# Edge counts of a graph layer in three narrow groups of tiles per window in place of one wide group

## The reference, cut to what matters

```python
xr = jnp.einsum('nd,rdf->rnf', x, W)
oi = xr[etype, dst]
oj = xr[etype, src]
qi = oi @ q
kj = oj @ k
alpha = jax.nn.leaky_relu(qi + kj, NEG_SLOPE)
m = jax.ops.segment_max(alpha, dst, num_segments=n_nodes)
e = jnp.exp(alpha - m[dst])
z = jax.ops.segment_sum(e, dst, num_segments=n_nodes)
a = e / (z[dst] + EPS)
msg = (a[:, :, None] * oj.reshape(-1, heads, out_ch)).reshape(-1, heads * out_ch)
out = jax.ops.segment_sum(msg, dst, num_segments=n_nodes)
```

## Time and profile before

| | |
|---|---|
| median of three executions | 1820.09 us (1813.9 to 1828.2) |
| the profiled execution | 1833.56 us |
| its span, first to last instruction | 1831.8 us (1.76 us lie outside) |
| granted clock of TensorE, mean | 0.939 |
| busy: PE, DVE, ACT, POOL | 1654.2, 1320.8, 771.8, 194.3 us |
| L1721, count matmuls, x840 | 136.2 us busy |
| L1283, oh_q, x420 | 185.9 us busy |
| L1285, oh_p, x420 | 105.4 us busy |

### The profile page before, as it was taken

How to read it: one execution, slowest core, us unless ns; L and a number is a source line. 1 busy time by engine, 2 the same in 40 slices (tenths; PEclk the granted TensorE clock), 3 DMA queues, 4 the chain that set the end, 5 groups by cost and what they waited for, 6 DMA issues and landing times.

```text
span 1831.8 us, 35065 instructions
## 1 busy us (share of the span) xinstructions
PE 1654.2 (90%) x10647; PEld 1216.5 (66%) x10648; DVE 1320.8 (72%) x2623; ACT 771.8 (42%) x1018; POOL 194.3 (11%) x256
## 2 busy tenths in 40 slices
PE   2699999999899999959999999958988899999966
PEld 2466676778765566649999999955545455555535
DVE  6778877765733899948899898952575277777786
ACT  2232112221202566448888888942211133333342
POOL 2200000000000000000000000001110033333334
PEclk9899999986789999979999999978989999999988
DMA  4111105223262544361103133023555351011202
GB/s 163 60 46 55 55 29 143 77 71 95 71 267 82 172 147 133 112 211 41 44 28 113 58 105 101 20 86 109 174 178 188 95 189 51 1 51 51 95 28 85
DMA packets 122827, 177.67 MB, mean 97 GB/s; under 512 B 12604, under 2 KB 96452, under 8 KB 122232
## 3 DMA queue, kind: packets, MB, share of 16 engines
q1 hardware_dynamic: 122744, 176.61, 30.0%
HBM read 118.75 MB, written 57.84 MB: 96 GB/s over the span
## 4 chain that ended last, share of the span: by engine, by line
PE 69%; DVE 13%; issue 9%; DMA 5%; ACT 2%; POOL 1%; SPq 1%; DVEq 1%; ACTq 0%; POOLq 0%
PE ps L1932 21%; PE ps L1721 7%; PE ps L1990 6%; PE ps L1989 6%; PE ps L1703 6%; PE ps L1704 5%; PE ps L1705 5%; DVE tt_junk L1431 4%; PE ps L1785 3%; PE ps L1764 3%; DMA x_d<-ev 1%; PE ps L1806 1%; PE ps L1714 1%; DVE w_lo L1293 1%; PE ps L1746 1%
## 5 line engine op out<-in xcount | busy, mean ns | idle before, releaser
L1932 PE MATMUL ps<-xrh,pf 128*128 (+1 forms) x2400 | 399.9, 330 | 24.8 <-DVE pf L1521 24.8
L1932 PEld LDWEIGHTS ps<-xrh,pf 128*128 128x128 f32 x2400 | 393.5, 191 | 31.3 <-issue 28.8
L1703 PE MATMUL ps<-w_hi,xt_hi 128*128 128x384 f16 x600 | 200.5, 334 | 24.0 <-DVE ev L1565 19.5
L1283 DVE TENSOR_SCALAR oh_q<-pat,codeT,neg_w 125x630 f16<-125x630 uint16 x420 | 185.9, 443 | 50.2 <-PE ps L1721 44.0
L1989 PE MATMUL ps<-x,ph 128*128 (+1 forms) x600 | 196.7, 328 | 20.3 <-POOL pl L862 20.3
L1521 DVE SCALAR_TENSOR_TENSOR pf<-vb,CT 128x1260 f32<-128x1260 f32 x120 | 175.8, 1468 | 35.2 <-PE ps L1932 35.2
L1704 PE MATMUL ps<-w_lo,xt_hi 128*128 128x384 f16 x600 | 200.5, 334 | 0.0
L1705 PE MATMUL ps<-w_hi,xt_lo 128*128 128x384 f16 x600 | 200.0, 333 | 0.0
L1990 PE MATMUL ps<-x,ph 128*128 (+1 forms) x600 | 198.0, 330 | 0.0
L1517 DVE SCALAR_TENSOR_TENSOR vb<-vb,tb 128x1260 f32<-128x1260 f32 x120 | 172.9, 1467 | 29.9 <-DMA b_bc<-in_L_gnn_b 20.7
L1431 DVE CUSTOM_DVE_ANT_0 tt_junk<-kbc,mb 126x1260 bf16<-126x1260 f32 x120 | 168.3, 1468 | 17.5 <-issue 16.0
(11 more groups left out here) (228 smaller groups left out, 2533.1 us busy)
## 6 DMA issues: line engine op xcount, KB each, us to landing
qbc<-tq_d SPq DMA_DIRECT2D x12, 1260.0 KB, 6.4
wst<-in_L_gnn_W SPq DMA_DIRECT2D x12, 1152.0 KB, 7.2
xr_d<-ev SPq DMA_DIRECT2D x60, 192.0 KB, 2.1
xrh<-xr_d SPq DMA_DIRECT2D x4, 2880.0 KB, 14.9
x_d<-ev SPq DMA_DIRECT2D x60, 192.0 KB, 2.3
x<-x_d SPq DMA_DIRECT2D x3, 3840.0 KB, 12.2
mb_d<-mb SPq DMA_DIRECT2D x30, 310.1 KB
mb<-mb_d SPq DMA_DIRECT2D x30, 310.1 KB
```

What stands on the lines that cost most here:

```text
L1283: dve.tensor_scalar(oh_q[0:ET, u, :], pat[0:ET, :], codeT[0:ET, ds(t0 + u, 1)], neg_w[0:ET, ds(w, 1)], ALU.subtract, ALU.is_equal)
L1703: pe.matmul(ps[:, bank, 0:CW], a_hi, hi[:, k, :], start=(k == 0), stop=False)
L1932: mm = pe.matmul(out[b], pf[j][:, b * DB:b * DB + P], x, start=(first and b % 2 == 0), stop=False, skip_group_check=True)
```

## The change

For ScalarE, SyncE and the store a window of 21 destinations is still one unit of 630 columns, but it is counted in three thirds of 7 destinations (WS), each with its own start tile and TG = 3 tiles of 125 edges. An oh_q has 210 columns (QS), those of its third, and a tile of a third needs one matmul of 210 columns. In PSUM the thirds stand 256 words apart, two in the first bank and one in the second. There are three semaphores of each kind, one for each third. So a window has nine oh_q, nine oh_p and nine count matmuls. A tile in which two thirds meet is taken twice, once in each; for the seeded edges no third touches more than three tiles, so count is 1 in every window again. The table has two 32-bit words a window: the start of the first third with count and first, and the starts of the second and third; VectorE reads both (window_thirds), TensorE only the first. The preparation of the table on VectorE works on three pairs of bounds a window. ScalarE reads PSUM in three pieces and writes the old order.

```diff
 KN = WN * R
 QN = NB * KN
-QH = QN // 2
+WS = 7
+NS = WN // WS
+KS = WS * R
+QS = NB * KS
+PS_STEP = 256
...
-TG = 7
-PARTS_OF = ((0, 2), (2, 4), (4, 6), (6, 7))
+TG = 3
...
-        oh_q = place("oh_q", [P, TG, QN], F16, 190720)
-        oh_p = place("oh_p", [P, TG, P], F16, 200800)
+        oh_q = place("oh_q", [P, NS, TG, QS], F16, 190720)
+        oh_p = place("oh_p", [P, NS, TG, P], F16, 194528)
...
 
         def window(eng, w):
 
-            word = eng.value_load(tabrow[0:1, ds(w, 1)], min_val=0, max_val=(NWN * MAXG << 16) + (MAXG << 9) + NT)
-            tile0 = eng.snap(word & 511, min_val=0, max_val=NT - 1)
+            word = eng.value_load(tabrow[0:1, ds(w, 1), 0], min_val=0, max_val=(NWN * MAXG << 16) + (MAXG << 9) + NTP)
+            tile0 = eng.snap(word & 511, min_val=0, max_val=NTP - TG)
             count = eng.snap((word >> 9) & 127, min_val=1, max_val=MAXG)
             first = eng.snap(word >> 16, min_val=0, max_val=NWN * MAXG)
             return tile0, count, first
+
+        def window_thirds(eng, w):
+
+            tile0, count, first = window(eng, w)
+            word = eng.value_load(tabrow[0:1, ds(w, 1), 1], min_val=0, max_val=(NTP << 16) + NTP)
+            tile1 = eng.snap(word & 511, min_val=0, max_val=NTP - TG)
+            tile2 = eng.snap(word >> 16, min_val=0, max_val=NTP - TG)
+            return (tile0, tile1, tile2), count, first
 
         W_K, W_V, W_S, W_Q = 0, NB, 3 * NB, 3 * NB + 3
         W_A = W_Q + 3 * K6 + 1
...
 
                 act.wait_ge(ct_cnt, w + 1)
                 act.wait_ge(ct_out[u], 16 * stored + 16)
-                act.activation(stage[u][:, :].rearrange("p (q n) -> p q n", q=2), ps[:, bank:bank + 2, 0:QH], ACT.Copy).then_inc(ct_ev, 1)
+                act.activation(stage[u][:, :].rearrange("p (q s d) -> p s q d", s=NS, d=WS),
+                               ps[:, bank:bank + 2, :].rearrange("p b (s n) -> p (b s) n", n=PS_STEP)[:, 0:NS, 0:QS].rearrange("p s (q d) -> p s q d", d=WS),
+                               ACT.Copy).then_inc(ct_ev, 1)
 
             for c in range(2):
                 with act.Fori(0, NB // 2) as ii:
...
 
             dve.wait_ge(e_const, 1)
             dve.wait_ge(e_row, 1)
-            dve.tensor_scalar(wrk[:, :], srow[:, 0, :], wlo[:, 1:2], None, ALU.is_le).then_inc(e_row, 1)
+            for a in range(NS):
+                last = dve.tensor_scalar(wrk[:, a, :], srow[:, 0, :], wlo[:, a, 1:2], None, ALU.is_le)
+            last.then_inc(e_row, 1)
             dve.wait_ge(e_row, 2)
-            dve.scalar_tensor_tensor(ovl[:, :], srow[:, 1, :], wlo[:, 0:1], wrk[:, :], ALU.is_ge, ALU.mult).then_inc(e_row, 1)
+            for a in range(NS):
+                last = dve.scalar_tensor_tensor(ovl[:, a, :], srow[:, 1, :], wlo[:, a, 0:1], wrk[:, a, :], ALU.is_ge, ALU.mult)
+            last.then_inc(e_row, 1)
             dve.wait_ge(e_row, 3)
-            dve.scalar_tensor_tensor(srow[:, 0, :], ovl[:, :], -1000.0, tix[:, 1, :], ALU.mult, ALU.add)
-            dve.tensor_tensor(srow[:, 1, :], ovl[:, :], tix[:, 0, :], ALU.mult).then_inc(e_row, 1)
+            dve.scalar_tensor_tensor(wrk[:, :, :], ovl[:, :, :], -1000.0, tix[:, 1:2, :].to_broadcast([NTAB, NS, NT]), ALU.mult, ALU.add)
+            dve.tensor_tensor(ovl[:, :, :], ovl[:, :, :], tix[:, 0:1, :].to_broadcast([NTAB, NS, NT]), ALU.mult).then_inc(e_row, 1)
             dve.wait_ge(e_row, 4)
-            dve.tensor_reduce(tab[:, 3:4], srow[:, 0, :], AX.X, ALU.min)
-            dve.tensor_reduce(tab[:, 4:5], srow[:, 1, :], AX.X, ALU.max).then_inc(e_row, 1)
+            dve.tensor_reduce(tab[:, 0:3], wrk[:, :, :], AX.X, ALU.min)
+            dve.tensor_reduce(tab[:, 3:6], ovl[:, :, :], AX.X, ALU.max).then_inc(e_row, 1)
             dve.wait_ge(e_row, 5)
-            dve.tensor_scalar(tab[:, 0:1], tab[:, 3:4], float(NT - 1), None, ALU.min).then_inc(e_base, 1)
+            dve.tensor_scalar(tab[:, 0:3], tab[:, 0:3], float(NT - 1), None, ALU.min).then_inc(e_base, 1)
             dve.wait_ge(e_base, 1)
-            dve.tensor_tensor(tab[:, 5:6], tab[:, 4:5], tab[:, 0:1], ALU.subtract).then_inc(e_base, 1)
+            dve.tensor_tensor(tab[:, 3:6], tab[:, 3:6], tab[:, 0:3], ALU.subtract).then_inc(e_base, 1)
             dve.wait_ge(e_base, 2)
-            dve.tensor_scalar(tab[:, 6:7], tab[:, 5:6], 1.0, float(TG // 2), ALU.max, ALU.add).then_inc(e_base, 1)
+            dve.tensor_reduce(tab[:, 6:7], tab[:, 3:6], AX.X, ALU.max).then_inc(e_base, 1)
             dve.wait_ge(e_base, 3)
-            dve.tensor_scalar(tab[:, 7:8], tab[:, 6:7], 1.0 / TG, MAGIC, ALU.mult, ALU.add).then_inc(e_base, 1)
+            dve.tensor_scalar(tab[:, 7:8], tab[:, 6:7], 1.0, float(TG // 2), ALU.max, ALU.add).then_inc(e_base, 1)
             dve.wait_ge(e_base, 4)
-            dve.tensor_scalar(tab[:, 1:2], tab[:, 7:8], MAGIC, None, ALU.subtract).then_inc(e_row, 1)
+            dve.tensor_scalar(tab[:, 8:9], tab[:, 7:8], 1.0 / TG, MAGIC, ALU.mult, ALU.add).then_inc(e_base, 1)
+            dve.wait_ge(e_base, 5)
+            dve.tensor_scalar(tab[:, 9:10], tab[:, 8:9], MAGIC, None, ALU.subtract).then_inc(e_row, 1)
+            dve.wait_ge(e_row, 6)
+            dve.tensor_scalar(tab[:, 10:11], tab[:, 9:10], -float(TG), float(NTP), ALU.mult, ALU.add).then_inc(e_base, 1)
+            dve.wait_ge(e_base, 6)
+            dve.tensor_scalar(tab[:, 11:14], tab[:, 0:3], tab[:, 10:11], None, ALU.min).then_inc(e_base, 1)
+            dve.wait_ge(e_base, 7)
+            dve.scalar_tensor_tensor(tab[:, 16:17], tab[:, 9:10], 512.0, tab[:, 11:12], ALU.mult, ALU.add)
+            dve.tensor_copy(tab[:, 18:20], tab[:, 12:14])
             dve.wait_ge(e_tr, 2)
-            dve.wait_ge(e_row, 6)
-            dve.scalar_tensor_tensor(tab[:, 6:7], tab[:, 1:2], 512.0, tab[:, 0:1], ALU.mult, ALU.add)
-            dve.tensor_copy(tab[:, 7:8], ps[0:NTAB, 4, 0:1]).then_inc(e_base, 1)
-            dve.wait_ge(e_base, 5)
-            dve.tensor_copy(tabi[:, :].bitcast(U16), tab[:, 6:8]).then_inc(e_row, 1)
+            dve.tensor_copy(tab[:, 17:18], ps[0:NTAB, 4, 0:1]).then_inc(e_base, 1)
+            dve.wait_ge(e_base, 8)
+            dve.tensor_copy(tabi[:, :].bitcast(U16), tab[:, 16:20]).then_inc(e_row, 1)
             dve.wait_ge(x_in, 32)
 
             def row_stats(src, j, n, mean_var, rows=P):
...
                         lo_half(2 * ii + j, j, hf)
 
 
-            for i in range(len(PARTS_OF)):
+            for i in range(NS):
                 dve.sem_inc(oh_free[i], 1)
 
-            def one_hots(w, tile0, count, first):
+            def one_hots(w, tiles, count, first):
                 with dve.Fori(0, count) as jj:
                     n1 = dve.snap(first + jj + 1)
-                    t0 = nc.s_assert_within(tile0 + TG * jj, 0, NTP - TG, skip_runtime_bounds_check_because="tile0 + TG * count <= NT + TG - 1 for every window of the table")
-                    for i, (u0, u1) in enumerate(PARTS_OF):
-                        dve.wait_ge(oh_free[i], n1)
-                        for u in range(u0, u1):
-                            dve.tensor_scalar(oh_q[0:ET, u, :], pat[0:ET, :], codeT[0:ET, ds(t0 + u, 1)], neg_w[0:ET, ds(w, 1)],
-                                              ALU.subtract, ALU.is_equal)
-                            last = dve.tensor_scalar(oh_p[0:ET, u, :], iota_l[0:ET, :], sloT[0:ET, ds(t0 + u, 1)], None, ALU.is_equal)
-                        last.then_inc(oh_rdy[i], 1)
+                    for a in range(NS):
+                        neg = neg_w[0:ET, ds(NS * w + a, 1)]
+                        t0 = dve.snap(nc.s_assert_within(tiles[a] + TG * jj, 0, NTP - TG, skip_runtime_bounds_check_because="tile + TG * count <= NTP for every third of a window in the table"))
+                        codes, slots = codeT[0:ET, ds(t0, TG)], sloT[0:ET, ds(t0, TG)]
+                        dve.wait_ge(oh_free[a], n1)
+                        for u in range(TG):
+                            dve.tensor_scalar(oh_q[0:ET, a, u, :], pat[0:ET, :], codes[:, u:u + 1], neg, ALU.subtract, ALU.is_equal)
+                            last = dve.tensor_scalar(oh_p[0:ET, a, u, :], iota_l[0:ET, :], slots[:, u:u + 1], None, ALU.is_equal)
+                        last.then_inc(oh_rdy[a], 1)
 
             def w_lo_part(c):
 
...
                 dve.tensor_tensor(w_lo[c % 2][:, :, :], wst[c % 2][:, :, :], w_hi[c % 2][:, :, :], ALU.subtract).then_inc(w_lo_done, 1)
 
             def count_part(w):
-                one_hots(w, *window(dve, w))
+                one_hots(w, *window_thirds(dve, w))
 
             dve.wait_ge(bias_in, 32)
             dve.wait_ge(tab_in, 16)
...
             def count_window(w, bank, count, first):
 
                 pe.wait_ge(ct_ev, w + 1)
-                for q in range(2):
-                    pe.matmul(ps[:, bank + q, 0:QH], ident16[:, :], zrow[:, :], start=True, stop=False, skip_group_check=True)
+                area = ps[:, bank:bank + 2, :].rearrange("p b (s n) -> p (b s) n", n=PS_STEP)[:, 0:NS, 0:QS]
```

(16 more changed lines are left out.)

46 lines of the change are left out of this document (23 added, 23 removed).

## The result

The changed kernel takes 1834.8 us (median of 9 runs, 1826.4 to 1840.6) beside 1818.0 for the kernel before. The medians lie 16.8 us apart; the ratio on record is 1.0063, 95% interval 1.0034 to 1.0093, and a second comparison gave 1.0079 (1.0053 to 1.0105). So it is slower by 0.6 to 0.8%, 11 to 14 us (0.9% by the medians). The forecast was 1815.3, 0.3% faster. The measured time is inside the range and within the 1% called no change, but it lies clearly on the other side of 1: the sum said -4.8 us and +11 to +14 came, 16 to 19 us more.

What follows compares the result with a forecast made beforehand. TensorE, busy 90%, was taken as the bound, with VectorE close behind in the V stage. Stage terms summed to -4.8 us, 1828.8 in the profiled execution's terms, 1815.3 for the median; range 1780 to 1848.

Steps and rivals of the forecast that it cites:

- start (table): Table preparation before the windows: about 4.4 us more work, partly taken back by the layer norm; +1.7 us, bounds +1 to +4.4.
- S: Three windows beside KV's sum: VectorE has air there, so -1.5 us, bounds -3 and 0.
- Q1 and Q2: Query stage, 18 windows: +1 us for the first three rounds, -2 for the others, together -1; bounds -19 and +6.
- VectorE takes over as the bound: Rival for K, V and query windows: at a pair of 0.50 us, +34 us in sum, 1854 us; chance 0.21.
- the table's words are read behind it, 0.45 back: K stage: next ev_t follows KF at once, table reads come behind it, saving 0.45 us; window 7.95 us, not 8.4.
- VectorE no longer waits for the product: V stage: table words are read while V and the last one-hots still run; window 5.2 us, taken as 5.35.
- TensorE needs 4.1: V stage, 20 windows: TensorE's need per window after the change, 4.1 us, where a window took 5.15.
- rival 3: K and V stages: TensorE, now waiting in each window, gets the lower clock in part; +15 us, 1830 or more; chance 0.04.
- waiting is not what lowered it there: Argument from the query stage: its clock of 0.91 came with TensorE busy 98% of the time.
- 0.34 + 0.78 of uncovered head ... I take 5.35: V window on VectorE: 3.69 us of pairs, the head, 0.2 and 0.2 make 5.2, taken as 5.35; +4 us over 20 windows.
- the +3 for w_lo: V stage: w_lo of 2.55 us comes twice, partly hidden by TensorE's backlog before; 1.5 us more each time, +3.
- so the matmuls' saving is kept, and the mean clock of 0.73 makes it no smaller: Block loop, nine windows: VectorE idle 39%, so -1.1 us each, -10 us; bounds -14 and -6.

Runs made afterwards that it cites:

- filler: Changed kernel, with TensorE adding matmuls of zeros (210 columns) in its V-stage idle time; ratio 1.0019 to the kernel before, V stage 120.0 us.
- pe_fixed: Changed kernel, with TensorE taking count and first as constants instead of reading the table; ratio 1.0017 to the kernel before, V stage 117.8 us.
- before_two_words: Kernel before, with VectorE's sequencer reading the window's word twice; ratio 0.999 to the unedited kernel before, V stage 112.4 us.

## Why the prediction was wrong, by its steps

The mean of three executions of the changed kernel less the mean of four of the kernel before, by stage, beside the forecast:

| | forecast | measured |
|---|---|---|
| start (table) | +1.7 | +1.5 |
| K | -1 | -1.4 |
| V | +7 | +14.3 |
| S | -1.5 | -2.9 |
| Q1 and Q2 | -1 | -4.2 |
| block loop | -10 | -1.2 |
| rest | 0 | +2.7 |
| sum | -4.8 | +8.7 |

(The means of before hold the first profile with its long block loop. Without it the block loop is 63.7 us before and the difference +3.3, Q is -5.2, start +1.7 and rest +3.0, and the sum is +12.8; the timed runs show 11 to 14.)

**Right.** The matmul of 210 columns at 0.095 us and TensorE's 1.05 a window (K windows begin at 6.97 for 8.06). The narrow oh_q at 334 ns and the pair at 0.41. The rule of the Trainium skill ("VectorE: DVE Perf Modes", "The TRN2 errata") that each small instruction pays its fixed latency held, 252 ns for 128 elements again, and its table's figure did not (by it 115 ns for 210 elements, an estimate; measured 334). The table's preparation: the layer norm starts at 26.14 for 21.78, 4.36 us later against 4.4, and 1.5 of it arrive at window 0. VectorE's second word: a load of 292 ns, and the head behind a waiting V is 2.21 us for 1.37, against 0.78 + 1.37. That VectorE takes over as the bound.

**Right by luck, the K stage, -1 against -1.4.** The mean of 7.9 us a window against 7.95 is made of two kinds: the first closing matmuls come 6.97, 6.97 and 7.53 us apart, the six others 8.3 in the mean. The step "the table's words are read behind it, 0.45 back" did not come: the head behind ev_t is 2.19 us, whole, and from ev_t to ev_t it is 8.26 us, more than the 8.06 before.

```profile
138.62 0.56 DVE L1334 TENSOR_TENSOR ev_t<-ps,bk_bc 128x384 f32<-128x384 f32 x1
140.81 0.34 DVE L1309 TENSOR_SCALAR oh_q<-pat,codeT,neg_w 125x210 f16<-125x210 uint16 x1 [1.64 <-issue]
...
146.88 0.56 DVE L1334 TENSOR_TENSOR ev_t<-ps,bk_bc 128x384 f32<-128x384 f32 x1
```

VectorE's lag does not show in K's closing matmuls. It shows in V, whose first addition comes 10.2 us behind window 9's closing, where it came 6.1 behind it before.

**Wrong, the V stage, +7 against +14.3.** The 7.3 us too few fall into three steps.
- "VectorE no longer waits for the product", and with it "TensorE needs 4.1". It counted TensorE's matmuls and left out TensorE's sequencer and its clock. Before, the branch and the table's word of the next window were read while a dozen matmuls stood queued. Once TensorE waits for the last one-hots nothing is queued, and 1.26 us stand bare ahead of the product. On top of it comes rival 3, to which 0.04 was given: TensorE's idle time lowered its clock in V to 0.94, a product then takes some 1.7 us longer (eleven matmuls at 0.32 for 0.16), V waits for it, and a window is 6.6 to 7.0 us and not 5.6. filler, which takes the spells away, is 3.1 to 4.1 us shorter from the first V to the last (some 3.5 of the 7.3); pe_fixed, which takes the read away and leaves the clock at 0.94, gave 4.2 us of V back. With either edit V hardly waits for products any more (0.2 and 1.3 us), so here it took both, the bare read and the spell, to make VectorE wait. The two gains are then largely the same microseconds; no run has both edits, so that part is argued. The argument against the rival ("waiting is not what lowered it there") was about another stage, in which the clock fell with TensorE busy; it said nothing on V.
- VectorE's own window, "0.34 + 0.78 of uncovered head ... I take 5.35". Where V waits for no product it is 5.3 to 5.9 us from V to V, 5.6 in the mean, with the pairs as forecast and a head of 1.6 to 2.3. The sequencer, not the engine, is full: it has no time to read the words ahead, so most of the head stays uncovered. Against that, the +3 for w_lo did not come: in the first profile the four intervals with it and behind it are as long as before (22.9 for 22.8 us together). In all VectorE's own work added some 8 us between the first and the last V (filler has 107.9 for 99.8), 1 more than the 7 of the sum, with terms that were wrong in both directions.
- The lag that K leaves behind, above: V's first addition is 4.1 us later after window 9's closing, and the last closing comes 1.4 us sooner after the last V, together +2.7. The sum had no term for it.

**Wrong, the block loop, -10 against +3 to -1.** The step "so the matmuls' saving is kept, and the mean clock of 0.73 makes it no smaller". The clock of 0.73 was that execution's, not the kernel's. The profiled execution was 13.5 us over the median and that was put in by scaling the sum by 0.74%, in place of asking in which stage it was longer. The saving can be seen where clocks are alike (before_two_words 76.7 at 0.78, changed 67.4 at 0.80), but three of the four profiles of the kernel before ran there at 0.92 to 0.97 and the three of the changed one at 0.79 to 0.84. Why the clock differs there was not taken apart, and whether the change lowers it stays open.

**Off by size.** The Q stage gained more than the -1, though its spread in the kernel before (136.3 to 145.2, against 134.9 to 135.1) is larger than the difference. The rest of the program, which has not changed, took 2.7 us more in the mean (1337.9 to 1344.9 for 1337.0 to 1340.7); three against four executions don't tell if that is chance.

## What to carry to other kernels

When a change takes work from the engine that bounds, look at what its sequencer does between two pieces of work as well: waits, branches and reads from a table were free here only as long as instructions that were ready stood queued in front of the engine, on both sides of a handshake. Add up the sequencer's own work for a round of the loop, as one adds up the engine's: here it was the longer of the two. Price a scalar read in front of a waiting instruction at its whole chain (here 0.6 to 0.8 us, sixty times), pack words, and read them ahead of the wait. A stage measured on one engine can hide another's lag until the next stage. And before a sum is made against one profiled execution that lies 0.7% over the median, find the stage that is long in it; with a second profile the stages that repeat (here to 0.1 us) and those that don't are told apart.

## What was not expected of the hardware

- In the changed kernel's V stage TensorE was idle for 25.9 of 122.6 us, in pieces such as 0.8 and 1.3 us, and was granted the lower clock in spells of some 3 us (product matmuls 0.32 us apart for 0.16), with a mean of 0.94 over 122 us; with TensorE kept busy on zeros it was 1.00.
- The same program's block loop had a mean granted clock of 0.72, 0.97, 0.92 and 0.92 in four executions, and took 81.5, 61.7, 64.6 and 64.6 us: 20 us of 1820 from the clock of one stage.
- Two edits that each brought 0.5 to 0.6% (1.0027 and 1.0017 for 1.0079) brought 0.6% together, and with a third, worth 1.6% alone, 2.1%.
